# Tree stage: PE's transposes and outputs of a tile between the logits of the next, and ScalarE's activations and copies in turn

## The chip, the cores and the metric

The kernel runs on one core of a Trainium2 chip. The metric is the device time of one execution in microseconds (us). Engines by the profile's names: PE (TensorE) multiplies matrices and transposes, PEld are its weight loads, ACT is ScalarE, DVE is VectorE, POOL is GpSimd, SP issues transfers.

## The reference

Two layers over x of shape (2, 1024, 128). Each layer adds an attention and a feed-forward part of the normalised x to x. The second layer's feed-forward part is a forest of 8 binary trees of 255 nodes, and this stage alone is changed:

```python
logits = x @ W_in.T + b_in                      # 2048 rows, 8 * 255 = 2040 columns
decisions = (logits > 0)                        # per row, tree and node
acts = silu(logits)
# from the root, 7 times: go to the child that the node's decision names;
# dmap is 1 at the 8 nodes of a tree's path, 0 elsewhere
out = (acts * dmap).reshape(B, WIDTH) @ W_out.T # 2040 -> 128
```

## The kernel before

The program is a row of stages, each in a block of its own: the projections, attention and experts of layer 0, the projections of layer 1, the trees (`walk_trees`, lines 1999 to 2175), the attention of layer 1. No instruction of a stage runs beside another stage's.

The trees work on NT = 16 tiles of 128 rows. For tile t:

- POOL copies the 128 columns of the transposed input into `xt` (line 2039).
- PE computes the logits, 128 x 2040, into the four banks of `ps_l`, in four chunks of 512 columns (504 in the last). A chunk is a small bf16 product that adds the bias (line 2058) and the float32 product (line 2059, two passes). Two chunks are a half, and `l_ready` counts halves. There is only one `ps_l`: a half of the next tile waits until ACT has read this tile's (`silu_ready`).
- DVE compares a half with zero (line 2143, "decision", `dec_ready`), twice; then walks the path down the trees with 14 small products and differences (lines 2151 and 2152, "path"); then multiplies the activations by the path (line 2159, "mask", `masked`).
- ACT applies Silu to a half, from `ps_l` into `act_v` (line 2105), behind DVE's decision on the same half. `act_v` has two buffers, one for each of two tiles.
- PE transposes the masked activations, 16 blocks in four groups of four ("T0" to "T3", line 2072), into the two buffers of `ps_t` (`t_ready`). ACT copies each group to SBUF (`mT`, two buffers; lines 2113, 2115 and 2116: "copy 0" to "copy 3", `t_read`). PE multiplies the copied blocks by W_out and sums all 16 in `ps_f` (line 2083, "outputs 0" to "outputs 3"; four blocks are eight passes).
- DVE adds `ps_f` to x (line 2164).

Each engine has its instructions in one written order and waits on semaphores. The stage is turned by one tile: between tiles t-1 and t, PE's order is all four chunks of tile t, then transposes and outputs of tile t-1, which begin with a wait for its mask. ACT's order is both Silus of tile t, then the four copies of tile t-1. DVE's order is decisions, path and mask of tile t, then the addition of tile t-1. Two such sections stand in the body of a loop that turns seven times; the first section and the last outputs are written out. "Section t" below is the part that has the logits of tile t and the outputs of tile t-1.

Of the kernel before, what the change touches and what calls it, by code (L numbers as in the profile page):

```python
# [9 lines left out]
ACT = mybir.ActivationFunctionType  # L10
# [4 lines left out]
P = 128  # L15
B, S, D = 2, 1024, 128
NT = B * S // P
# [27 lines left out]
NCH = (WIDTH + P - 1) // P  # L45
LASTW = WIDTH - (NCH - 1) * P
# [1952 lines left out]
def walk_trees(nc, g):  # L1999

    with ExitStack() as ctx:
        r = Room(nc, ctx, "ff")
        win, wout, bin32 = g.win, g.wout, g.bin32
        rest = r.sb("rest", [1, WIDTH])
        binp = r.sb("binp", [1, 3, WIDTH], BF16)
        bins = r.sb("bins", [3, WIDTH], BF16)
        xt = r.sb("xt", [P, 2, P])
        dec = r.sb("dec", [P, PAR, NODES], BF16)
        path = r.sb("path", [P, PAR, NODES], BF16)
        act_v = r.sb("act_v", [P, 2, WIDTH])  # L2010
        mT = r.sb("mT", [P, 2, CH])
        ps_l = r.ps("ps_l", [P, 4 * CH])
        ps_t = r.ps("ps_t", [P, 2, CH])
        ps_f = r.ps("ps_f", [P, CH])

        w_in, bias_ready, step = r.sem("w_in"), r.sem("bias_ready"), r.sem("step")
        x_ready, l_ready, dec_ready, silu_ready = r.sem("x_ready"), r.sem("l_ready"), r.sem("dec_ready"), r.sem("silu_ready")
        masked, t_ready, t_read, f_ready, f_read = (r.sem("masked"), r.sem("t_ready"), r.sem("t_read"), r.sem("f_ready"),
                                                    r.sem("f_read"))
        NCK = (NCH + 3) // 4  # L2020
        STEPS = 2 * DEPTH - 1
        HALVES = [(0, 2 * CH), (2 * CH, WIDTH)]
        BOUNDS = [(c * CH, min(CH, WIDTH - c * CH)) for c in range(4)]

        with nc.Block() as block:
            @block.sync
            def _(sp):
                sp.wait_ge(bias_ready, 4)
                for part in range(3):
                    sp.dma_start(bins[part:part + 1, :], binp[0:1, part, :]).then_inc(w_in, 16)  # L2030
                sp.wait_ge(w_in, 48)
# [15 lines left out]
            @block.tensor  # L2047
            def _(pe):
                pe.wait_ge(g.trees_in, 64)
                pe.wait_ge(w_in, 48)  # L2050

                def logits(t, p, first):
                    pe.wait_ge(x_ready, t + 1)
                    for x in range(2):
                        if not (first and p == 0):
                            pe.wait_ge(silu_ready, t * 2 + (x - 1))
                        for c, w in BOUNDS[2 * x:2 * x + 2]:
                            pe.matmul(ps_l[:, c:c + w], g.onesb[0:3, :], bins[:, c:c + w], start=True, stop=False)
                            m = pe.matmul(ps_l[:, c:c + w], xt[:, p, :], win[:, c:c + w], start=False, stop=True)
                        m.then_inc(l_ready, 1)  # L2060

                def outputs(t, p, first):
                    pe.wait_ge(masked, t + 1)
                    if not (first and p == 0):
                        pe.wait_ge(f_read, t)

                    def turn(x):
                        if not (first and p == 0 and x < 2):
                            pe.wait_ge(t_read, t * NCK + (x - 1))
                        for c in range(4 * x, min(4 * x + 4, NCH)):  # L2070
                            w = P if c < NCH - 1 else LASTW
                            m = pe.transpose(ps_t[0:w, x % 2, (c % 4) * P:(c % 4 + 1) * P],
                                             act_v[:, p, c * P:c * P + w], g.ident[:, :])
                        m.then_inc(t_ready, 1)

                    turn(0)
                    for x in range(NCK):
                        if x + 1 < NCK:
                            turn(x + 1)
                        pe.wait_ge(t_read, t * NCK + (x + 1))  # L2080
                        for c in range(4 * x, min(4 * x + 4, NCH)):
                            w = P if c < NCH - 1 else LASTW
                            m = pe.matmul(ps_f[:, 0:P], mT[0:w, x % 2, (c % 4) * P:(c % 4 + 1) * P],
                                          wout[0:w, c, :], start=(c == 0), stop=(c == NCH - 1))
                        if x == NCK - 1:
                            m.then_inc(f_ready, 1)

                logits(0, 0, True)
                logits(1, 1, True)
                outputs(0, 0, True)  # L2090
                with pe.Fori(1, NT // 2) as i:
                    logits(i * 2, 0, False)
                    outputs(i * 2 - 1, 1, False)
                    logits(i * 2 + 1, 1, False)
                    outputs(i * 2, 0, False)
                outputs(NT - 1, 1, False)

            @block.scalar
            def _(act):
                def silu(t, p, first):  # L2100
                    if not first:
                        act.wait_ge(t_ready, (t - 1) * NCK)
                    for x, (lo, hi) in enumerate(HALVES):
                        act.wait_ge(dec_ready, t * 2 + (x + 1))
                        act.activation(act_v[:, p, lo:hi], ps_l[:, lo:hi], ACT.Silu).then_inc(silu_ready, 1)

                def turned(t, p, first):
                    for x in range(NCK):
                        act.wait_ge(t_ready, t * NCK + (x + 1))

                        full = 4 * P if x < NCK - 1 else (NCH - 1 - 4 * x) * P
                        if x < NCK - 1:
                            act.activation(mT[:, x % 2, 0:full], ps_t[:, x % 2, 0:full], ACT.Copy).then_inc(t_read, 1)
                        else:
                            act.activation(mT[:, x % 2, 0:full], ps_t[:, x % 2, 0:full], ACT.Copy)
                            act.activation(mT[0:LASTW, x % 2, full:full + P], ps_t[0:LASTW, x % 2, full:full + P],
                                           ACT.Copy).then_inc(t_read, 1)

                silu(0, 0, True)
                silu(1, 1, True)  # L2120
                turned(0, 0, True)
                with act.Fori(1, NT // 2) as i:
                    silu(i * 2, 0, False)
                    turned(i * 2 - 1, 1, False)
                    silu(i * 2 + 1, 1, False)
                    turned(i * 2, 0, False)
                turned(NT - 1, 1, False)

            @block.vector
            def _(dve):  # L2130
# [171 lines left out]
```

## Time and profile before

| | us |
|---|---|
| median of 3 runs | 2088.07 (2087.74 to 2088.33) |
| execution that was profiled | 2088.2 |
| its span | 2086.5 |
| the tree stage in it, from the first logits to the last addition | 827.32 to 1053.56 |

The page gives the kernel as a whole, with PE busy 84% of the span, DVE 72%, ACT 64% and POOL 30%. The tree stage is a ninth of the span, and none of its lines is among the costliest groups; it is read by windows and by the timeline of a stretch. In a timeline each line is a run of like instructions: start, duration, engine, line, operation, output and inputs, count, and in brackets how long the engine was idle ahead of it and what ended that. The durations of PE's groups overlap those of the next, so what PE needs for a group is read from start to start. PE's granted clock is a share of 2.4 GHz; its two levels are 1.0 and 0.5, and a mean between them is a mix.

### The profile page before, as it was taken

How to read it: one execution, taken by the hardware profiler on the slowest of the kernel's cores; microseconds unless marked ns; L12 is line 12 of the kernel's file. 1: busy time of each engine (PE TensorE's matmuls, PEld its weight loads, DVE VectorE, ACT ScalarE, POOL GpSimd, SP SyncE). 2: the span in 40 equal slices, each digit the busy share in tenths (PEclk: the TensorE clock that was granted, in tenths of full speed). 3: DMA queues.
4: the chain of work that ended last, by engine and by line, in shares of the span. 5: the costliest groups of instructions: out<-in, count | busy, mean ns of one | idle time of the engine just before them, and what ended most of it. 6: DMA issues, size and time to landing. Idle time of an engine off the chain costs nothing. (4 is left out here: it accounts for less than half of the span.)

```text
span 2086.5 us, 35986 instructions
## 1 busy us (share of the span) xinstructions
PE 1760.6 (84%) x10131; PEld 1056.3 (51%) x10163; DVE 1497.3 (72%) x4721; ACT 1327.3 (64%) x2819; POOL 619.0 (30%) x1540
## 2 busy tenths in 40 slices
PE   5699999999978895888865888888889838988877
PEld 2345555577756443555532555555555525555544
DVE  4588888311133555777747899999999969999974
ACT  3177777533321521233347999999999939999983
POOL 0045454000000441000014444444444414444440
PEclk8599999999985997999987999999999969999988
DMA  6200000100010220000020110111100101011000
GB/s 168 82 21 22 23 23 16 41 1 0 0 50 0 81 91 31 0 0 0 0 64 11 31 32 16 31 31 31 31 24 23 31 16 28 18 31 31 21 18 15
DMA packets 38186, 61.77 MB, mean 30 GB/s; under 512 B 10225, under 2 KB 15347, under 8 KB 38004
## 3 DMA queue, kind: packets, MB, share of 16 engines
q1 hardware_dynamic: 38069, 60.51, 9.8%
q8 instruction: 36, 0.59, 0.1%
q14 instruction: 81, 0.66, 0.1%
HBM read 34.14 MB, written 17.83 MB: 25 GB/s over the span
## 5 line engine op out<-in xcount | busy, mean ns | idle before, releaser
L1629 ACT ACTIVATE a_trash<-a_sc,a_search 128x1024 bf16<-128x1024 f32 (+7 forms) x768 | 586.2, 767 | 74.6 <-POOL a_search L1568 31.7
L1384 PE MATMUL a_ps_s<-a_k,a_q 128*128 128x512 f32 (+3 forms) x768 | 311.1, 520 | 64.4 <-DVE a_sc L1845 51.1
L1418 PE MATMUL a_ps_o<-a_kT,a_v 128*65 128x512 f32 (+3 forms) x768 | 287.5, 498 | 53.7 <-ACT a_kT L1646 52.5
L1402 PE MATMUL a_ps_t<-g_ident,a_sc 128*128 128x128 f32 x1152 | 228.5, 285 | 20.9 <-ACT a_kT L1646 18.9
L1845 DVE TENSOR_SCALAR_CACHE_REDUCE a_sc<-a_ps_s,g_search 128x1024 f32<-128x1024 f32 (+7 forms) x256 | 207.9, 812 | 23.3 <-PE a_ps_s L1386 16.1
L585 DVE TENSOR_REDUCE a_top<-a_ps_row 128x1 f32<-128x512 f32 (+3 forms) x384 | 196.7, 553 | 24.6 <-PE a_ps_row L423 18.9
L1384 PEld LDWEIGHTS a_ps_s<-a_k,a_q 128*128 128x128 f32 x768 | 132.3, 196 | 160.0 <-issue 100.6
L1805 DVE SCALAR_TENSOR_TENSOR a_below<-a_sc,a_found 128x768 f32<-128x768 f32 (+7 forms) x256 | 211.3, 835 | 1.1
L1404 PE MATMUL a_ps_t<-a_minus,a_short 128*128 128x128 bf16 x1152 | 211.8, 221 | 0.0
L1402 PEld LDWEIGHTS a_ps_t<-g_ident,a_sc 128*128 128x128 f32 x1152 | 164.5, 143 | 92.0 <-ACT a_kT L1646 47.1
L549 ACT ACTIVATE a_prob<-a_ps_col 128x1024 f32<-128x1024 f32 (+7 forms) x256 | 159.2, 650 | 68.7 <-PE a_ps_col L436 65.5
L1646 ACT ACTIVATE a_kT<-a_ps_t 128x512 f32<-128x512 f32 x288 | 162.0, 583 | 24.9 <-PE a_ps_t L1404 17.7
L1418 PEld LDWEIGHTS a_ps_o<-a_kT,a_v 128*65 128x65 f32 x768 | 89.0, 140 | 164.5 <-ACT a_kT L1646 103.3
L741 ACT ACTIVATE ex_hid<-ex_ps_h,le_b 128x512 f32<-128x512 f32 x128 | 87.5, 687 | 128.1 <-PE ex_ps_h L718 127.8
L1818 DVE MAX8 a_best<-a_below 128x8 f32<-128x160 f32 (+5 forms) x576 | 157.2, 328 | 1.1
L1629 ACT ACTIVATION_READ_ACCUMULATOR a_trash<-a_sc,a_search 128x1 f32 x768 | 148.0, 193 | 0.0
L792 DVE SCALAR_TENSOR_TENSOR l_acc<-ex_ps_y,l_comb,l_acc 128x128 f32 x112 | 31.9, 345 | 151.4 <-PE ex_ps_y L709 151.1
L1639 ACT ACTIVATE a_short<-a_sc,a_cutoff 128x128 bf16<-128x128 f32 (+2 forms) x192 | 110.8, 655 | 44.9 <-DVE a_cutoff L1865 44.9
L1404 PEld LDWEIGHTS a_ps_t<-a_minus,a_short 128*128 128x128 bf16 x1152 | 123.7, 107 | 19.4 <-issue 19.4
L709 PEld LDWEIGHTS ex_ps_y<-le_w,ex_hid 128*128 128x128 f32 x1024 | 118.7, 192 | 13.4 <-issue 13.4
L709 PE MATMUL ex_ps_y<-le_w,ex_hid 128*128 128x128 f32 x1024 | 118.8, 275 | 0.0
L420 PE MATMUL a_ps_row<-a_k,a_q 128*128 128x512 bf16 (+3 forms) x353 | 114.7, 335 | 4.8 <-DVE a_top L585 2.7
(267 smaller groups left out, 3336.1 us busy)
## 6 DMA issues: line engine op xcount, KB each, us to landing
a_v<-g_v SPq DMA_DIRECT2D x32, 260.0 KB, 2.3
q1turned<-p_full SPq DMA_DIRECT2D x32, 256.0 KB, 2.0
a_q<-q1turned SPq DMA_DIRECT2D x32, 256.0 KB, 3.6
a_k<-k1turned SPq DMA_DIRECT2D x32, 256.0 KB, 4.0
stack<-p_parts SPq DMA_DIRECT2D x24, 256.0 KB, 3.7
a_q<-stack SPq DMA_DIRECT2D x32, 96.0 KB, 2.2
a_k<-stack SPq DMA_DIRECT2D x32, 96.0 KB, 2.2
le_w<-d_w SPq DMA_DIRECT2D x1, 2048.0 KB, 8.5
```

The source lines that it names most:

```text
L549: act.activation(prob[:, p, PO[j]:PO[j] + S - j * P], ps_col[:, col_buffer(n, p, j), 0:S - j * P], ACT.Exp, scale=SCALE).then_inc(col_read, 1)
L585: dve.tensor_reduce(top[:, i, c:c + 1], ps_row[:, bank, 0:width], AX.X, ALU.max).then_inc(row_read, 1)
L709: m = pe.matmul(ps_y[:, e % 2, t, :], hid[:, e % 2, hc, t * P:(t + 1) * P], w2[:, e, hc, :], start=(hc == 0), stop=(hc == HC - 1))
L1384: pe.matmul(ps_s[:, j % 2, c:c + w], q[:, p, i * P:width], k[:, p, c:c + w], start=True, stop=True)
L1402: pe.matmul(out, columns(h, i)[:, c * P:(c + 1) * P], g.ident[:, :], is_transpose=True, start=True, stop=False)
L1404: m = pe.matmul(out, short[:, OFF[i] + c * P:OFF[i] + (c + 1) * P], minus[:, :], start=False, stop=True)
L1418: m = pe.matmul(ps_o[0:VW1, lo // HALF, (lo % HALF) * P:CH], v[:, p, c, :], kT[:, u % 2, a * P:b * P], start=(c == 0), stop=(c == LAST[lo ...
L1629: act.activation(trash[:, u % 2, 0:(i + 1) * P], columns(h, i), ACT.Sign, scale=-1.0, bias=trials[:, p, c, i:i + 1], accum_out=balance[:, ...
L1646: act.activation(kT[:, u % 2, :], ps_t[:, u % 2, :], ACT.Exp).then_inc(t_read, 1)
L1805: lane[i] = did(dve.scalar_tensor_tensor(lows(i), columns(hs, i), found[:, i:i + 1], columns(hs, i), ALU.is_le, ALU.mult))
L1818: did(dve.max(best[:, p, i, a, :], buf[:, a * w:(a + 1) * w]))
L1845: dve.tensor_scalar(columns(h + 1, i), ps_s[:, j % 2, 0:(i + 1) * P], shift.rearrange("p n i -> p (n i)"), None, ALU.subtract, ALU.max, ac ...
```

## The change

PE: the logits of tile t are split around the first transposes of tile t-1. After three of the four chunks PE waits for the mask of tile t-1 and makes T0; then comes the fourth chunk, then T1, outputs 0, T2, outputs 1, T3, outputs 2, outputs 3. The wait for `f_read` (the addition of the tile before) moves from ahead of the transposes to ahead of outputs 0. ACT: the copies of tile t-1 and the Silus of tile t take turns: copy 0, Silu 0, copy 1, Silu 1, copy 2, copy 3. The orders of DVE, POOL and SP, all buffers and all instructions stay. The first section is now like the others, with the four chunks of tile 1 split in the same way.

```diff
--- before.py
+++ after.py
@@ -2049,82 +2049,105 @@
                 pe.wait_ge(g.trees_in, 64)
                 pe.wait_ge(w_in, 48)
 
-                def logits(t, p, first):
+                def half(t, p, x):
+                    for c, w in BOUNDS[2 * x:2 * x + 2]:
+                        pe.matmul(ps_l[:, c:c + w], g.onesb[0:3, :], bins[:, c:c + w], start=True, stop=False)
+                        yield pe.matmul(ps_l[:, c:c + w], xt[:, p, :], win[:, c:c + w], start=False, stop=True)
+
+                def turn(t, p, first, x):
+                    if not (first and x < 2):
+                        pe.wait_ge(t_read, t * NCK + (x - 1))
+                    for c in range(4 * x, min(4 * x + 4, NCH)):
+                        w = P if c < NCH - 1 else LASTW
+                        m = pe.transpose(ps_t[0:w, x % 2, (c % 4) * P:(c % 4 + 1) * P],
+                                         act_v[:, p, c * P:c * P + w], g.ident[:, :])
+                    m.then_inc(t_ready, 1)
+
+                def output(t, p, first, x):
+                    if x == 0 and not first:
+                        pe.wait_ge(f_read, t)
+                    pe.wait_ge(t_read, t * NCK + (x + 1))
+                    for c in range(4 * x, min(4 * x + 4, NCH)):
+                        w = P if c < NCH - 1 else LASTW
+                        m = pe.matmul(ps_f[:, 0:P], mT[0:w, x % 2, (c % 4) * P:(c % 4 + 1) * P],
+                                      wout[0:w, c, :], start=(c == 0), stop=(c == NCH - 1))
+                    if x == NCK - 1:
+                        m.then_inc(f_ready, 1)
+
+                def logits(t, p, first, x, both):
                     pe.wait_ge(x_ready, t + 1)
-                    for x in range(2):
-                        if not (first and p == 0):
-                            pe.wait_ge(silu_ready, t * 2 + (x - 1))
-                        for c, w in BOUNDS[2 * x:2 * x + 2]:
-                            pe.matmul(ps_l[:, c:c + w], g.onesb[0:3, :], bins[:, c:c + w], start=True, stop=False)
-                            m = pe.matmul(ps_l[:, c:c + w], xt[:, p, :], win[:, c:c + w], start=False, stop=True)
-                        m.then_inc(l_ready, 1)
-
-                def outputs(t, p, first):
-                    pe.wait_ge(masked, t + 1)
-                    if not (first and p == 0):
-                        pe.wait_ge(f_read, t)
-
-                    def turn(x):
-                        if not (first and p == 0 and x < 2):
-                            pe.wait_ge(t_read, t * NCK + (x - 1))
-                        for c in range(4 * x, min(4 * x + 4, NCH)):
-                            w = P if c < NCH - 1 else LASTW
-                            m = pe.transpose(ps_t[0:w, x % 2, (c % 4) * P:(c % 4 + 1) * P],
-                                             act_v[:, p, c * P:c * P + w], g.ident[:, :])
-                        m.then_inc(t_ready, 1)
-
-                    turn(0)
-                    for x in range(NCK):
-                        if x + 1 < NCK:
-                            turn(x + 1)
-                        pe.wait_ge(t_read, t * NCK + (x + 1))
-                        for c in range(4 * x, min(4 * x + 4, NCH)):
-                            w = P if c < NCH - 1 else LASTW
-                            m = pe.matmul(ps_f[:, 0:P], mT[0:w, x % 2, (c % 4) * P:(c % 4 + 1) * P],
-                                          wout[0:w, c, :], start=(c == 0), stop=(c == NCH - 1))
-                        if x == NCK - 1:
-                            m.then_inc(f_ready, 1)
-
-                logits(0, 0, True)
-                logits(1, 1, True)
-                outputs(0, 0, True)
+                    if not first:
+                        pe.wait_ge(silu_ready, t * 2 + (x - 1))
+                    chunks = half(t, p, x)
+                    next(chunks)
+                    if both:
+                        next(chunks).then_inc(l_ready, 1)
+                    return chunks
+
+                def section(t, p, first):
+                    u, q = t - 1, 1 - p
+                    logits(t, p, False, 0, True)
+                    second = logits(t, p, False, 1, False)
+                    pe.wait_ge(masked, t)
+                    turn(u, q, first, 0)
+                    next(second).then_inc(l_ready, 1)
+                    turn(u, q, first, 1)
+                    output(u, q, first, 0)
+                    turn(u, q, first, 2)
+                    output(u, q, first, 1)
+                    turn(u, q, first, 3)
+                    output(u, q, first, 2)
+                    output(u, q, first, 3)
+
+                logits(0, 0, True, 0, True)
+                logits(0, 0, True, 1, True)
+                section(1, 1, True)
                 with pe.Fori(1, NT // 2) as i:
-                    logits(i * 2, 0, False)
-                    outputs(i * 2 - 1, 1, False)
-                    logits(i * 2 + 1, 1, False)
-                    outputs(i * 2, 0, False)
-                outputs(NT - 1, 1, False)
+                    section(i * 2, 0, False)
+                    section(i * 2 + 1, 1, False)
+                pe.wait_ge(masked, NT)
+                turn(NT - 1, 1, False, 0)
+                for x in range(NCK):
+                    if x + 1 < NCK:
+                        turn(NT - 1, 1, False, x + 1)
+                    output(NT - 1, 1, False, x)
 
             @block.scalar
             def _(act):
-                def silu(t, p, first):
-                    if not first:
+                def silu(t, p, first, x):
+                    lo, hi = HALVES[x]
+                    if x == 0 and not first:
                         act.wait_ge(t_ready, (t - 1) * NCK)
-                    for x, (lo, hi) in enumerate(HALVES):
-                        act.wait_ge(dec_ready, t * 2 + (x + 1))
-                        act.activation(act_v[:, p, lo:hi], ps_l[:, lo:hi], ACT.Silu).then_inc(silu_ready, 1)
-
-                def turned(t, p, first):
-                    for x in range(NCK):
-                        act.wait_ge(t_ready, t * NCK + (x + 1))
-
-                        full = 4 * P if x < NCK - 1 else (NCH - 1 - 4 * x) * P
-                        if x < NCK - 1:
-                            act.activation(mT[:, x % 2, 0:full], ps_t[:, x % 2, 0:full], ACT.Copy).then_inc(t_read, 1)
-                        else:
-                            act.activation(mT[:, x % 2, 0:full], ps_t[:, x % 2, 0:full], ACT.Copy)
-                            act.activation(mT[0:LASTW, x % 2, full:full + P], ps_t[0:LASTW, x % 2, full:full + P],
-                                           ACT.Copy).then_inc(t_read, 1)
-
-                silu(0, 0, True)
-                silu(1, 1, True)
-                turned(0, 0, True)
+                    act.wait_ge(dec_ready, t * 2 + (x + 1))
+                    act.activation(act_v[:, p, lo:hi], ps_l[:, lo:hi], ACT.Silu).then_inc(silu_ready, 1)
+
+                def turned(t, x):
+                    act.wait_ge(t_ready, t * NCK + (x + 1))
+                    full = 4 * P if x < NCK - 1 else (NCH - 1 - 4 * x) * P
+                    if x < NCK - 1:
+                        act.activation(mT[:, x % 2, 0:full], ps_t[:, x % 2, 0:full], ACT.Copy).then_inc(t_read, 1)
+                    else:
+                        act.activation(mT[:, x % 2, 0:full], ps_t[:, x % 2, 0:full], ACT.Copy)
+                        act.activation(mT[0:LASTW, x % 2, full:full + P], ps_t[0:LASTW, x % 2, full:full + P],
+                                       ACT.Copy).then_inc(t_read, 1)
+
+                def section(t, p, first):
+                    u = t - 1
+                    turned(u, 0)
+                    silu(t, p, first, 0)
+                    turned(u, 1)
+                    silu(t, p, first, 1)
+                    turned(u, 2)
+                    turned(u, 3)
+
+                silu(0, 0, True, 0)
+                silu(0, 0, True, 1)
+                section(1, 1, True)
                 with act.Fori(1, NT // 2) as i:
-                    silu(i * 2, 0, False)
-                    turned(i * 2 - 1, 1, False)
-                    silu(i * 2 + 1, 1, False)
-                    turned(i * 2, 0, False)
-                turned(NT - 1, 1, False)
+                    section(i * 2, 0, False)
+                    section(i * 2 + 1, 1, False)
+                for x in range(NCK):
+                    turned(NT - 1, x)
 
             @block.vector
             def _(dve):
```

## Rows read from the trace of the kernel before

**Rows 1.** The page: the span.

```profile
span 2086.5 us, 35986 instructions
```

**Rows 2.** Windows: busy us by engine (instructions), then PE's granted clock, DMA share, GB/s.

```profile
868.00:1046.00 178.00, 151.84 (x780) 98.56 (x779) 128.95 (x235) 55.58 (x91) 3.23 (x11) 0.96 0.00 0
...
881.02:895.82 14.80, 12.83 (x62) 8.73 (x61) 11.19 (x19) 4.28 (x7) 0.29 (x1) 0.88 0.00 0
...
844.00:854.00 10.00, 8.18 (x43) 7.73 (x44) 9.35 (x17) 4.28 (x7) 0.00 (x0) 0.58 0.00 0
```

**Rows 3.** Timeline, one section: start, duration, engine, line, operation [idle before <- releaser].

```profile
908.97 0.38 PE L2058 MATMUL ff_ps_l<-ff_bins,g_onesb 3*128 3x512 bf16 x1
...
913.09 0.38 PE L2058 MATMUL ff_ps_l<-ff_bins,g_onesb 3*128 3x504 bf16 x1
...
914.35 1.04 PE L2072 MATMUL ff_ps_t<-g_ident,ff_act_v 128*128 128x128 f32 x8
...
914.55 1.22 DVE L2143 TENSOR_SCALAR ff_dec<-ff_ps_l 128x1016 bf16<-128x1016 f32 x1 [1.50 <-PE ff_ps_l L2059]
...
915.80 1.02 ACT L2105 ACTIVATE ff_act_v<-ff_ps_l 128x1016 f32<-128x1016 f32 x1 [1.70 <-DVE ff_dec L2143]
...
916.71 1.08 ACT L2113 ACTIVATE ff_mT<-ff_ps_t 128x512 f32<-128x512 f32 x2
...
917.36 1.16 PE L2083 MATMUL ff_ps_f<-l_wout,ff_mT 128*128 128x128 f32 x8 [1.97 <-ACT ff_mT L2113]
...
918.35 0.60 PE L2072 MATMUL ff_ps_t<-g_ident,ff_act_v 128*128 128x128 f32 x4
...
919.68 0.60 PE L2072 MATMUL ff_ps_t<-g_ident,ff_act_v 128*128 128x128 f32 x4
...
920.12 2.07 PE L2083 MATMUL ff_ps_f<-l_wout,ff_mT 128*128 128x128 f32 x16
...
920.32 0.49 ACT L2115 ACTIVATE ff_mT<-ff_ps_t 128x384 f32<-128x384 f32 x1 [0.73 <-PE ff_ps_t L2072]
...
921.20 2.29 DVE L2159 TENSOR_TENSOR ff_act_v<-ff_act_v,ff_path 128x2040 f32<-128x2040 f32 x1
...
922.12 0.38 PE L2058 MATMUL ff_ps_l<-ff_bins,g_onesb 3*128 3x512 bf16 x1
```

**Rows 4.** Timeline of the stage's start, to the first transposes of tile 1.

```profile
827.32 0.58 PE L2058 MATMUL ff_ps_l<-ff_bins,g_onesb 3*128 3x512 bf16 x1 [17.03 <-DMA ff_bins<-ff_binp]
...
829.83 0.60 PE L2058 MATMUL ff_ps_l<-ff_bins,g_onesb 3*128 3x512 bf16 x1
...
841.62 2.28 DVE L2159 TENSOR_TENSOR ff_act_v<-ff_act_v,ff_path 128x2040 f32<-128x2040 f32 x1
...
843.96 1.97 PE L2072 MATMUL ff_ps_t<-g_ident,ff_act_v 128*128 128x128 f32 x8 [3.52 <-DVE ff_act_v L2159]
...
849.62 1.06 PE L2072 MATMUL ff_ps_t<-g_ident,ff_act_v 128*128 128x128 f32 x4
...
850.47 1.91 PE L2083 MATMUL ff_ps_f<-l_wout,ff_mT 128*128 128x128 f32 x8
...
852.18 0.69 PE L2072 MATMUL ff_ps_t<-g_ident,ff_act_v 128*128 128x128 f32 x4
...
860.10 1.04 PE L2072 MATMUL ff_ps_t<-g_ident,ff_act_v 128*128 128x128 f32 x8
```

**Rows 5.** Timeline of the stage's end.

```profile
1037.64 1.04 PE L2072 MATMUL ff_ps_t<-g_ident,ff_act_v 128*128 128x128 f32 x8
...
1044.51 2.28 DVE L2159 TENSOR_TENSOR ff_act_v<-ff_act_v,ff_path 128x2040 f32<-128x2040 f32 x1
...
1047.09 1.06 PE L2072 MATMUL ff_ps_t<-g_ident,ff_act_v 128*128 128x128 f32 x8 [1.61 <-DVE ff_act_v L2159]
...
1053.27 0.29 DVE L2164 TENSOR_TENSOR g_x<-g_x,ff_ps_f 128x128 f32<-128x128 f32 x1 [6.29 <-PE ff_ps_f L2083]
```

**Rows 6.** Line 2105 of ScalarE: table loads, ns min/median/max, first and last start.

```profile
L2105 ACT ACT_TABLE_LOAD  x1: 1283/1283/1283, 816.2 to 816.2; - x1
```

## The prediction

> **What bounds the kernel now.** The page first: its span is 2086.5 us [rows 1], and none of the stage's lines is among its costliest groups. So I cut out the stage with the view of windows: from 868 to 1046 us PE is busy 151.8 of 178 us, DVE 129.0, ACT 55.6 [rows 2]. No engine is full, so the order of the work sets the time. The timeline of one section shows that order [rows 3]. At 908.97 PE starts the logits of a tile; the last of four chunks starts at 913.09, and the transposes of the tile before at 914.35. Then PE idles 1.97 us, to 917.36, until ACT has copied the first transposes. That copy stands on ACT behind both Silu halves, the second Silu waits for DVE's second decision (914.55 to 915.80), and this waits for the last logits. After the copy PE works without a real break, to the next logits at 922.12: 13.15 us for a tile. DVE idles ahead of that second decision, 1.50 us, for the same logits. The loop PE, DVE, ACT, PE is closed, and closes once a tile.
>
> Not every tile takes 13.15. The section from 881.02 takes 14.80, with a mean granted clock of 0.88 [rows 2], so 0.12 x 14.80 / 0.5 = 3.6 us of it at 1.2 instead of 2.4 GHz. It lies right behind the wait for the copy. From the first transposes of tile 1 (860.10) to those of tile 14 (1037.64) there are 13 intervals: 177.54 us, or 13.66 each [rows 4, 5]. 13 x 13.15 is 170.95, and the other 6.59 is four times the excess of 1.65 us: four sections had the slow stretch. The rest of the kernel lies in blocks of its own before and behind this one, and the next block's first loads are issued after this stage's last addition (1053.56) [rows 5]: nothing of it can hide in this stage or be hidden by it.
>
> **The change part by part.** No instruction is added or removed: a tile has the same 16 transposes, 32 output passes, four chunks, two Silus and five copies. No DMA moves. All durations therefore come from rows of before, and the sum is one of order. It is made against this profile's own execution (2088.2 us, its span and 1.7 around it), which lies 0.1 over the median of the runs.
>
> I call a the start of a section's first transposes.
>
> *DVE's branch.* The last chunk of logits now follows the first transposes, and these wait for the mask of the tile before. First transposes: 0.44 us for four (919.68 to 920.12). Start of a chunk to start of the decision on it: 1.46 (913.09 to 914.55). Decision and path together 6.65 (914.55 to 921.20), of which the decision is 1.25, to the start of its Silu at 915.80; the mask 2.29 [rows 3]. From the mask's end to the transposes that wait for it: 0.06 at one place (843.90 to 843.96), 0.30 at another (1046.79 to 1047.09, behind the end of the loop) [rows 4, 5]; I take 0.10, since inside the loop PE stands at the wait already. Sum: 0.44 + 1.46 + 6.65 + 2.29 + 0.10 = 10.94 us. The first decision (1.25, after an addition of 0.29 [rows 5]) fits between the mask's end and a + 1.90, with some 0.4 us idle; its logits were done at the section's start. This is the wait that the change adds: behind PE's wait for the mask now stand the last chunk and all outputs, and DVE's second decision waits for that chunk. On ACT, copy 0 now stands ahead of Silu 0, which so waits for the mask too; who needs Silu 0 (the next tile's logits, the mask) is 5 us away or more. POOL's copy of the input tile is allowed a tile ahead as before and costs nothing.
>
> *PE's branch.* T0 0.44, last chunk 1.26 (913.09 to 914.35), T1 0.44, outputs 0 0.99 (917.36 to 918.35), T2 and outputs 1 1.33 (918.35 to 919.68), T3 0.44, outputs 2 and 3 2.00 (920.12 to 922.12, with a small wait for the last copy in it), then three chunks of the next tile, 1.37 + 1.37 + 1.26 = 4.00 (a third of 908.97 to 913.09 is 1.37) [rows 3]. Sum 10.90. This holds if no copy is late. From the start of four transposes to the copy: 0.64 us (919.68 to 920.32). Copy 0: a + 0.64 to a + 1.24; outputs 0 start at a + 2.14, so the stall of 1.97 us is gone. Silu 0 starts behind the first decision, at a + 1.5, done at a + 2.5; copy 1 (transposes at a + 1.70) to about a + 3.1, needed at a + 3.57. Silu 1 starts with the end of the second decision, a + 3.15, to a + 4.15; copy 2 to a + 4.75, needed at a + 4.90: the narrowest place, 0.15 us. Copy 3 as now. PE is then at the next wait at a + 10.90 and the mask is done at a + 10.84: both engines are at their limit, and what is late next is either, by a few hundredths.
>
> So an interval is 10.94 us where the trace has 13.15 to 14.80. Its bounds: 10.90 with the short release; 11.14 with the long one; 11.3 if copy 2 besides misses its time by 0.15. The nearest rows give the short one, so I stay at 10.94.
>
> *The clock.* PE's idle time in a section falls from about 2.0 us in one piece to some 0.1 to 0.2 in two or three. The low stretches began right behind that piece, so I expect none of the four: that gain is in the 10.94. Should they stay, PE has no reserve to hide them, and 4 x 1.65 = 6.6 us are lost again.
>
> *Start.* Transposes of tile 0 still wait for its mask (843.96), with a longer idle ahead of them (PE stops one chunk earlier), and the clock is low there: 0.58 from 844 to 854 [rows 2]. At that clock four transposes take 0.85 (849.62 to 850.47), eight output passes 1.71 (to 852.18), a chunk 2.51 (827.32 to 829.83) [rows 4]. New section 1: 0.85 + 2.51 + 0.85 + 1.71 + 0.85 + 1.71 = 8.5, at 852.4, where the clock rose in the trace; then 0.44 + 2.0 and three chunks (4.0): transposes of tile 1 at 858.9, 1.2 us before 860.10. The last chunk of tile 1 is late by this (decision at 847.4, not 845), but its mask ends at 856.4, early enough. If PE's unbroken work brings the clock up sooner, up to 2.5 us more; if later, up to 1 less.
>
> *End.* Before, the last section's transposes and those of tile 15 are 9.45 us apart (1037.64 to 1047.09); now this is an interval like the others, a loss that stands in the sum by counting 14 intervals. The tail from 1047.09 to the end of the last addition, 1053.56, is 6.47 and unchanged [rows 5].
>
> *Sum.* 858.9 + 14 x 10.94 + 6.47 = 1018.5, against 1053.56: 35.0 us. 2088.2 - 35.0 = 2053.2 us; against the median it is 2053.1.
>
> **The rivals.**
> *The low clock stays in the loop (0.10).* For it: four of 14 sections have it, and section 1 is entered after a longer idle. Against: all four start behind a wait of 2 us that goes. Time: 2053.2 + 6.6 = 2059.8 us.
> *The hand-overs cost more (0.08).* Three engines now pass work within tenths of a microsecond; each late copy hits PE. With 0.5 us more an interval, 11.44: 2060.2 us. Against it: the hand-overs of rows 3 are of this kind already (the second decision is over at 915.77, its Silu starts at 915.80).
> *ScalarE reloads tables (0.02).* A section now goes between Silu and Copy four times, not twice. A load took 1.28 us [rows 6]. Two would stand between the second decision and copy 2: 2.56 less the margin of 0.15 is 2.4 an interval, 14 x 2.4 = 34: 2087 us, no change. Against it: one load in the whole stage for 32 Silus, and a Copy starts with no gap at the Silu's end (915.80 + 1.02, copy at 916.71).
> The Trainium skill ("ScalarE: Activation LUTs", section "What ACT_TABLE_LOAD costs") puts a switch of sets at 2.66 us with the drain, by which two would add 5.3 us to an interval and make the kernel slower by some 37 us; its section on table sets has Copy in every set, and with that the trace agrees.
> *The other side: PE sinks to the low clock for the stage (0.02).* The wait for the mask now stands in the middle of the logits, in every section, and section 1 begins cold. At 1.2 GHz a section is 4 x 2.51 + 4 x 0.85 + 4 x 1.71 = 20.3 us, 14 of them 284 against the 187.0 between 860.10 and 1047.09: 2185 us. It decides from a mean interval of (187.0 + 1.2) / 14 = 13.44, that is when over a quarter of the sections (2.5 of 9.4 us) run so. Against it: PE at the low clock would be busy without a break, and in the trace it rose in just such a stretch (844 to 854).
> That the change doesn't do what it says (an order on PE undone elsewhere) has no mechanism here: the queues take the order as written.
>
> **How the numbers follow.** 0.78 for the forecast, 0.10, 0.08, 0.02 and 0.02 for the rivals. Low end: 2050.5, the interval of 10.90 and 2 us more at the start. High end: 2061, which takes in either of the first two rivals (2059.8 and 2060.2), since the margin at copy 2 is small beside what the hand-overs leave open. A change within 0.2% (4 us, what can't be told from none here) has 0.02, slower 0.02, faster 0.96.
>
> **What would show it.** Right: starts of the first transposes 10.9 to 11.0 us apart; no wait of PE for a copy above some 0.2; DVE idle only about 0.4 us before the second decision; granted clock 1.00 from the second section on; the stage's last addition near 1018.6. Wrong: intervals of 11.3 and more with PE waiting for copy 1 or 2; sections with 0.88; table loads; or later stages that take longer than before, for which I see no cause.

## The result, and the profile after

The changed kernel takes 2055.09 us (median of 4 runs, 2052.08 to 2057.55), the one before 2088.20 (4 runs, 2087.74 to 2088.66). The ratio is 0.9841, with a 95% interval of 0.9824 to 0.9858: 33.1 us less, where 35.0 were forecast, and inside the range.

The page of the changed kernel: span, and busy time of each engine.

```profile
span 2050.4 us, 36006 instructions
...
PE 1755.8 (86%) x10163; PEld 1048.2 (51%) x10163; DVE 1495.6 (73%) x4721; ACT 1328.5 (65%) x2819; POOL 620.8 (30%) x1540
```

The busy times are those of before to 5 us in 1760 (PE), the span is 36.1 us shorter [rows 1]: what went was waiting and low clock. Where it went is read from the stage's windows; the columns are as in [rows 2].

```profile
core 0: us, PE busy (x) PEld busy (x) DVE busy (x) ACT busy (x) POOL busy (x), PEclk, DMA share, GB/s
...
860.00:1000.00 140.00, 139.81 (x754) 88.49 (x753) 122.99 (x228) 53.26 (x88) 3.26 (x11) 1.00 0.00 0
...
842.60:847.50 4.90, 4.85 (x14) 2.98 (x15) 2.32 (x2) 1.85 (x3) 0.30 (x1) 0.50 0.00 0
...
1011.50:1015.00 3.50, 3.46 (x16) 3.16 (x17) 0.19 (x1) 1.19 (x2) 0.00 (x0) 0.52 0.02 5
...
826.08:1019.25 193.17, 183.77 (x960) 116.01 (x960) 156.01 (x288) 69.29 (x112) 4.15 (x14) 0.96 0.00 0
```

From the first logits to the last addition the stage takes 193.17 us, 33.07 less than the 226.24 of before. The other two rows show where its clock is low: in section 1 (0.50 from 842.60 to 847.50) and at the last tile (0.52). The other 3.0 us of the span's difference lie outside the stage: it begins 1.24 earlier, and what follows it takes 1031.15 instead of 1032.94. No instruction differs there, and such differences come and go between the profiles of the kernels below. Between 860 and 1000 us the granted clock is 1.00; between 868 and 1046 it was 0.96 [rows 2].

One section of the changed kernel, in its timeline (start, duration, engine, line, operation, and in brackets the idle time before it):

```profile
907.49 0.39 PE L2054 MATMUL ff_ps_l<-ff_bins,g_onesb 3*128 3x512 bf16 x1
...
909.24 2.28 DVE L2182 TENSOR_TENSOR ff_act_v<-ff_act_v,ff_path 128x2040 f32<-128x2040 f32 x1
...
911.66 0.65 PE L2062 MATMUL ff_ps_t<-g_ident,ff_act_v 128*128 128x128 f32 x4
...
912.24 0.38 PE L2054 MATMUL ff_ps_l<-ff_bins,g_onesb 3*128 3x504 bf16 x1
...
912.35 0.60 ACT L2128 ACTIVATE ff_mT<-ff_ps_t 128x512 f32<-128x512 f32 x1 [6.00 <-PE ff_ps_t L2062]
...
912.89 1.03 ACT L2122 ACTIVATE ff_act_v<-ff_ps_l 128x1024 f32<-128x1024 f32 x1
...
913.50 0.60 PE L2062 MATMUL ff_ps_t<-g_ident,ff_act_v 128*128 128x128 f32 x4
...
913.70 1.22 DVE L2166 TENSOR_SCALAR ff_dec<-ff_ps_l 128x1016 bf16<-128x1016 f32 x1 [0.84 <-PE ff_ps_l L2055]
...
913.94 1.06 PE L2072 MATMUL ff_ps_f<-l_wout,ff_mT 128*128 128x128 f32 x8
...
914.96 1.02 ACT L2122 ACTIVATE ff_act_v<-ff_ps_l 128x1016 f32<-128x1016 f32 x1 [0.22 <-DVE ff_dec L2166]
...
915.87 0.59 ACT L2128 ACTIVATE ff_mT<-ff_ps_t 128x512 f32<-128x512 f32 x1
...
916.60 2.07 PE L2072 MATMUL ff_ps_f<-l_wout,ff_mT 128*128 128x128 f32 x16
...
918.60 0.39 PE L2054 MATMUL ff_ps_l<-ff_bins,g_onesb 3*128 3x512 bf16 x1
```

None of PE's lines has a bracket: the wait of 1.97 us before outputs 0 (913.94 here) is gone [rows 3]. A short wait for the mask is left ahead of T0, 0.2 us, too short for a bracket. The transposes T0, at 900.54, 911.66 and 922.76, are 11.11 us apart, and so are 12 of the 14 intervals to 0.02. ACT does copy, Silu, copy, Silu, copy, and its own waits (6.00 and 0.22 us) hold up neither PE nor DVE. The loop now runs through DVE: mask to 911.52, T0 at 911.66, last chunk at 912.24, second decision at 913.70, path, and the next mask.

The stage's start (section 1) and its end:

```profile
842.65 1.11 PE L2062 MATMUL ff_ps_t<-g_ident,ff_act_v 128*128 128x128 f32 x4 [4.87 <-DVE ff_act_v L2182]
...
843.70 0.60 PE L2054 MATMUL ff_ps_l<-ff_bins,g_onesb 3*128 3x504 bf16 x1
...
846.07 1.06 PE L2062 MATMUL ff_ps_t<-g_ident,ff_act_v 128*128 128x128 f32 x4
...
855.94 0.60 PE L2062 MATMUL ff_ps_t<-g_ident,ff_act_v 128*128 128x128 f32 x4
```

```profile
1011.54 1.97 PE L2062 MATMUL ff_ps_t<-g_ident,ff_act_v 128*128 128x128 f32 x8 [4.00 <-DVE ff_act_v L2182]
...
1013.44 1.81 PE L2072 MATMUL ff_ps_f<-l_wout,ff_mT 128*128 128x128 f32 x8
...
1018.96 0.29 DVE L2187 TENSOR_TENSOR g_x<-g_x,ff_ps_f 128x128 f32<-128x128 f32 x1 [7.27 <-PE ff_ps_f L2072]
```

Transposes of tile 1 start 29.86 us after the first logits (32.78 before). Those of tile 15 start behind 4.00 us of idle time, at a granted clock of 0.52, and eight passes take 1.81 us; from them to the end it is 7.71 us, where it was 6.47 [rows 5].

### The profile page after: what moved, and what is told of

Its sections match the earlier page's. It is cut to its first block and busy times, and to the rows that moved or that the text cites. A ratio compares the mean times of both kernels' runs of the same rounds, so it can differ in the third digit from the quotient of the medians.

```text
span 2050.4 us, 36006 instructions
## 1 busy us (share of the span) xinstructions
PE 1755.8 (86%) x10163; PEld 1048.2 (51%) x10163; DVE 1495.6 (73%) x4721; ACT 1328.5 (65%) x2819; POOL 620.8 (30%) x1540
## 5 line engine op out<-in xcount | busy, mean ns | idle before, releaser
L420 PE MATMUL a_ps_row<-a_k,a_q 128*128 128x512 bf16 (+3 forms) x384 | 124.2, 342 | 4.9 <-DVE a_top L585 2.7
L385 POOL TENSOR_SCALAR_AFFINE_SELECT a_prob<-a_prob 128x128 f32<-128x128 f32 x256 | 75.6, 296 | 144.6 <-POOLq L382 144.1
```

What stands on the lines that cost most here:

```text
L420: last = pe.matmul(ps_row[:, bank, 0:width], q[:, h, i * P:(i + 1) * P], k[:, h, c * CH:c * CH + width], start=True, stop=True)
```

## The experiments

All profiles are read by the same four numbers, in us: first logits to T0 of tile 1, interval between T0s in the loop, T0 of tile 15 to the end, and the whole stage. The kernel before was run alongside each series, with medians of 2088.20, 2087.84 and 2087.03 us; a ratio goes with the runs of its own series, so it isn't the quotient of two medians of this table.

| kernel | to T0 of tile 1 | interval | last tile | stage | median (runs) | ratio to before, 95% |
|---|---|---|---|---|---|---|
| before | 32.78 | 13.15, four of 14.80 | 6.47 | 226.24 | 2088.20 (4) | 1 |
| changed | 29.86 | 11.11 | 7.71 | 193.17 | 2055.09 (4) | 0.9841 (0.9824 to 0.9858) |
| changed, again | 33.32 | 11.12 | 7.88 | 196.88 | 2055.25 (5) | 0.9847 (0.9834 to 0.9861) |
| PE's order alone | 36.24 | 13.59, two of 16.31 and 15.15 | 6.56 | 234.74 | 2093.56 (8) | 1.0026 (1.0016 to 1.0037) |
| ACT's order alone | 30.06 | 11.51 | 7.58 | 196.66 | 2057.31 (4) | 0.9866 (0.9851 to 0.9882) |
| before, wait filled | 32.99 | 13.15, none longer | 7.55 | 220.96 | 2081.45 (8) | 0.9974 (0.9963 to 0.9985) |
| path without its last level | 29.10 | 10.91 | 8.20 | 188.58 | 2050.07 (2) | 0.9827 |
| without outputs 1 | 29.52 | 11.11 | 7.26 | 192.33 | 2054.01 (2) | 0.9846 |
| mask in halves | 30.71 | 10.91 | 7.77 | 190.30 | 2050.90 (5) | 0.9830 (0.9816 to 0.9843) |
| mask in halves, PE kept warm | 24.76 | 10.92 | 6.56 | 183.17 | 2043.26 (5) | 0.9792 (0.9778 to 0.9805) |

### Which of the two orders carries it

```diff
 # PE's order alone: ACT of the changed kernel as it was before
-                    turned(u, 0)
                     silu(t, p, first, 0)
-                    turned(u, 1)
                     silu(t, p, first, 1)
+                    turned(u, 0)
+                    turned(u, 1)
                     turned(u, 2)
```

> PE in the new order, ACT in the old one (both Silus, then the four copies). My theory, that the stall goes only if copy 0 no longer stands behind Silu 1: the second decision now comes later than before (behind T0), Silu 1 runs from a + 3.3 to a + 4.2, copy 0 to a + 4.8, so outputs 0 start 2.5 us later than in the changed kernel; an interval is 11.1 + 2.5 = 13.6 us, as long as before, and the low clock is there again in some sections. Time 2088 to 2096 us. Rival, PE's order carries the gain by itself: interval 11.1 to 11.5, time 2055 to 2061 us.

PE's timeline in this kernel:

```profile
899.74 0.38 PE L2054 MATMUL ff_ps_l<-ff_bins,g_onesb 3*128 3x512 bf16 x1
...
905.55 0.60 PE L2062 MATMUL ff_ps_t<-g_ident,ff_act_v 128*128 128x128 f32 x4
...
908.56 1.16 PE L2072 MATMUL ff_ps_f<-l_wout,ff_mT 128*128 128x128 f32 x8 [2.41 <-ACT ff_mT L2128]
...
913.33 0.39 PE L2054 MATMUL ff_ps_l<-ff_bins,g_onesb 3*128 3x512 bf16 x1
```

The wait for copy 0 has grown from 1.97 to 2.41 us, and an interval is 13.59 (logits start at 899.74 and at 913.33). Two sections had the low clock. The time is 0.26% above before, interval 0.16 to 0.37%: PE's new order by itself is a small loss. The rival is out.

The other half: the kernel before with the changed kernel's whole ACT block (copy 0, Silu 0, copy 1, Silu 1, copy 2, copy 3).

> ACT in the new order, PE in the old one (four chunks, then T0 and T1). My theory: outputs 0 need only copy 0, done at a + 1.24, against T1's end at a + 0.88, so 0.4 us of the stall of 1.97 is left; outputs 1 and 2 wait some tenths for copies 1 and 2, which stand behind the Silus. Interval 11.6 us, DVE idle twice a tile, no low clock, time 2060 to 2064 us: three quarters of the gain. Rival, each order is worth nothing without the other: interval 13.1 or more, time 2080 to 2090 us.

```profile
912.48 1.04 PE L2072 MATMUL ff_ps_t<-g_ident,ff_act_v 128*128 128x128 f32 x8
...
913.12 0.60 ACT L2111 ACTIVATE ff_mT<-ff_ps_t 128x512 f32<-128x512 f32 x1 [7.16 <-PE ff_ps_t L2072]
...
913.62 1.02 ACT L2105 ACTIVATE ff_act_v<-ff_ps_l 128x1024 f32<-128x1024 f32 x1
...
913.77 1.16 PE L2083 MATMUL ff_ps_f<-l_wout,ff_mT 128*128 128x128 f32 x8 [0.25 <-ACT ff_mT L2111]
...
915.00 1.04 ACT L2105 ACTIVATE ff_act_v<-ff_ps_l 128x1016 f32<-128x1016 f32 x1
...
915.89 0.63 ACT L2111 ACTIVATE ff_mT<-ff_ps_t 128x512 f32<-128x512 f32 x1
```

T0 and T1 start at 912.48, copy 0 at 913.12, Silu 0 behind it, outputs 0 at 913.77 after 0.25 us. The interval is 11.51, no section is long, and 2057.31 us were measured, somewhat better than the 2060 to 2064 expected. So ACT's order alone takes 1.64 of the 2.04 us of an interval and all of the low clock in the loop; PE's split of the logits adds the other 0.40, and only beside it. By medians the two kernels are 2 us apart and their 95% ranges overlap, so the times alone don't separate them. The traces do: each of 13 intervals is 0.40 longer with ACT's order alone, 5.2 us. But its last one is 1.57 shorter (9.44 against 11.01 us), because PE's old order has the last tile's logits all done ahead of the T0 that this interval is counted from, and so the two stages are 3.5 us apart (196.66 and 193.17).

### What the clock was worth

```diff
+                        if x == 0:
+                            pe.matmul(ps_w[:, :], g.ident[:, :], win[:, 0:CH], start=True, stop=True)
+                            for _ in range(2):
+                                pe.matmul(ps_w[:, :], g.onesb[0:3, :], bins[:, 0:CH], start=True, stop=True)
                         pe.wait_ge(t_read, t * NCK + (x + 1))
```

> The kernel before, with one float32 product of 512 columns and two small bf16 ones put on PE in front of outputs 0, results unused: they fill most of PE's wait of 1.97 us for copy 0. My theory, that this wait brings the low clock of four sections: all sections take 13.15 us, the stage 226.2 - 6.6 = 219.6 us, the time 2081.5 us, and 6.6 of the changed kernel's 33 us are the clock's. Rival, the low stretches have nothing to do with the wait (or the products overrun it): three to five long sections stay, time 2088 us or more.

First the kernel before, around its wait for copy 0 in the section from 881.02 (the wait ends at 889.4; columns as in [rows 2]):

```profile
886.00:890.00 4.00, 2.03 (x15) 1.51 (x13) 3.09 (x10) 2.15 (x4) 0.29 (x1) 0.99 0.00 0
889.90:893.30 3.40, 3.40 (x18) 3.40 (x18) 3.19 (x7) 0.60 (x1) 0.00 (x0) 0.50 0.00 0
```

PE's timeline of one section with the wait filled, and the window of the loop:

```profile
913.21 1.02 PE L2082 MATMUL ff_ps_w<-l_win,g_ident 128*128 128x512 f32 x2
...
914.17 0.60 PE L2084 MATMUL ff_ps_w<-ff_bins,g_onesb 3*128 3x512 bf16 x2
...
915.34 1.16 PE L2088 MATMUL ff_ps_f<-l_wout,ff_mT 128*128 128x128 f32 x8 [0.58 <-ACT ff_mT L2118]
```

```profile
860.00:1034.00 174.00, 165.91 (x845) 98.22 (x844) 130.75 (x243) 57.44 (x94) 3.55 (x12) 1.00 0.00 0
```

The extra products run from 913.21 to about 914.8 and outputs 0 wait 0.58 instead of 1.97 us. All 13 intervals are 13.15 us, the granted clock is 1.00, and the kernel is 0.26% faster for doing more work. The four long sections (6.6 us in the profile of before) were thus the wait's doing, through the clock. The time is the 2081.5 us forecast. The stage gained 5.3 us, because its last tile took 1.1 longer: there PE waited only 0.25 us for copy 0, and the extra products hold up outputs 0.

### What sets 11.11 us

```diff
 # path without its last level
-                    for d in range(DEPTH):
+                    for d in range(LEVELS):          # LEVELS = DEPTH - 1
```

> The changed kernel without the last of the seven levels of the path on DVE (two operations of 0.77 us a tile; the lowest nodes' part of the path is left at 1). My theory, that DVE's branch sets the interval of 11.11 and PE's is 0.2 behind it: the interval falls to PE's own sum, 0.53 + 1.26 + 0.44 + 0.89 + 0.44 + 0.89 + 0.44 + 2.00 + 1.38 + 1.37 + 1.26 = 10.90, not by the 1.55 taken away. Rival, PE binds already: it stays at 11.11. Second rival, PE is far from binding: 9.6.

```profile
900.39 0.60 PE L2063 MATMUL ff_ps_t<-g_ident,ff_act_v 128*128 128x128 f32 x4
...
902.38 1.22 DVE L2167 TENSOR_SCALAR ff_dec<-ff_ps_l 128x1016 bf16<-128x1016 f32 x1 [1.94 <-PE ff_ps_l L2056]
...
911.31 0.60 PE L2063 MATMUL ff_ps_t<-g_ident,ff_act_v 128*128 128x128 f32 x4
```

The interval is 10.91 to 10.92 (900.39 to 911.31 here), DVE has 1.94 us of idle time before its second decision, and PE is the loop: 1.55 us less on DVE bring 0.20.

```diff
 # without outputs 1
-                    for c in range(4 * x, min(4 * x + 4, NCH)):
+                    for c in range(4 * x, min(4 * x + 4, NCH)) if x != 1 else ():
```

> The changed kernel without the eight passes of outputs 1 on PE (0.89 us a tile). My theory: DVE's branch has nothing of them, the interval stays at 11.11 and PE waits some 1.0 us for the mask. Rival, PE binds: 10.2.

```profile
907.61 2.05 PE L2072 MATMUL ff_ps_f<-l_wout,ff_mT 128*128 128x128 f32 x16 [0.64 <-ACT ff_mT L2128]
...
909.59 0.39 PE L2054 MATMUL ff_ps_l<-ff_bins,g_onesb 3*128 3x512 bf16 x1
...
911.44 2.29 DVE L2182 TENSOR_TENSOR ff_act_v<-ff_act_v,ff_path 128x2040 f32<-128x2040 f32 x1
...
913.86 0.65 PE L2062 MATMUL ff_ps_t<-g_ident,ff_act_v 128*128 128x128 f32 x4
```

Without eight of its passes PE has 0.89 us less to do, yet T0s are 11.11 apart and T0 still comes 0.13 behind the mask's end (911.44 + 2.29 to 913.86). The wait for the mask is not the 1.0 us expected: 0.64 us of PE's new idle time goes to copy 2, since outputs 2 now follow T3 directly, and some 0.3 to the mask. Neither costs anything. Together: DVE's branch sets 11.11, and PE's limit is 10.91, 0.20 below.

### A version that beats both

```diff
-                    a = act_v[:, p, :]
-                    dve.tensor_tensor(a, a, path.rearrange("p a n -> p (a n)"), ALU.mult).then_inc(masked, 1)
+                    for x, (lo, hi) in enumerate(HALVES):
+                        dve.wait_ge(silu_ready, t * 2 + (x + 1))
+                        a = act_v[:, p, lo:hi]
+                        dve.tensor_tensor(a, a, path.rearrange("p a n -> p (a n)")[:, lo:hi],
+                                          ALU.mult).then_inc(masked, 1)
 ...
+                    if x in (0, 2):                  # ahead of T0 and of T2
+                        pe.wait_ge(masked, t * 2 + (1 + x // 2))
```

> The changed kernel with DVE's mask in two halves, so that T0 and T1 wait for the first 1024 columns alone, T2 for the rest. If DVE's branch binds by the wait of T0 for the whole mask, its loop shrinks by 1.1 us to 10.0, DVE's own work is 10.35, and PE's sum of 10.90 takes over: interval 10.90, stage 14 x 0.21 = 2.9 us shorter and 1.1 more at the last tile, time some 4 us below the changed kernel, 2051 us. Rival, the halves cost DVE more than they free (another 0.1 us and a hand-over on each): interval 11.1 to 11.2, no gain.

DVE and PE in this kernel:

```profile
921.65 2.35 DVE L2183 TENSOR_TENSOR ff_act_v<-ff_act_v,ff_path 128x1024 f32<-128x1024 f32 x2
...
923.92 0.60 PE L2064 MATMUL ff_ps_t<-g_ident,ff_act_v 128*128 128x128 f32 x4
```

T0 no longer waits (923.92, with the first half of the mask done about 1.1 us before), and PE's 10.91 is the interval. The halves cost DVE 2.35 us for two where one mask took 2.28. The median is 2050.90; beside the changed kernel's 2055.25 that is the expected 4 us, but the 95% ranges of the two ratios overlap, so the gain rests on the timeline: 0.2 us in each of 13 intervals and 1.1 in the last (11.01 to 9.92), 3.8 us in all. The stages of the changed kernel's two profiles are 2.9 and 6.6 us longer than this one; what differs from 3.8 is mostly the start.

```diff
+                def warm(n):
+                    for _ in range(n):
+                        pe.matmul(ps_w[:, :], g.ident[:, :], win[:, 0:CH], start=True, stop=True)
 ...
+                warm(8)        # ahead of the wait for the biases, before the first logits
+                    warm(3)    # section 1, ahead of T0
+                warm(2)        # ahead of T0 of tile 15
```

> As the kernel with the mask in halves, and float32 products of 512 columns, results unused, on PE where it has nothing to do: 8 ahead of the first logits, 3 ahead of T0 in section 1, 2 ahead of the last tile's T0. If the low clock at the start and the end of the stage comes from PE's idle time there: the first two chunks 1.37 instead of 2.5 us, T0, last chunk and T1 of section 1 at full clock (2 us), the tail 6.5 instead of 7.7: 5 us less, time 2046 us, and a narrower spread, since the start of the stage was what differed between the two profiles of the changed kernel (29.9 and 33.3 us from the first logits to T0 of tile 1). Rival, the products delay what waits behind them, or the clock falls all the same: no gain or a loss against the kernel with halves.

PE's timeline at the start of this kernel's stage (the unread products start at 816.21), and the window of its last T0:

```profile
816.21 9.92 PE L2052 MATMUL ff_ps_w<-l_win,g_ident 128*128 128x512 f32 x16 [5.94 <-PEq L870]
...
827.26 0.38 PE L2060 MATMUL ff_ps_l<-ff_bins,g_onesb 3*128 3x512 bf16 x1 [1.13 <-DMA ff_bins<-ff_binp]
...
828.63 0.39 PE L2060 MATMUL ff_ps_l<-ff_bins,g_onesb 3*128 3x512 bf16 x1
...
840.76 0.66 PE L2070 MATMUL ff_ps_t<-g_ident,ff_act_v 128*128 128x128 f32 x4 [1.26 <-DVE ff_act_v L2192]
...
852.02 0.60 PE L2070 MATMUL ff_ps_t<-g_ident,ff_act_v 128*128 128x128 f32 x4
```

```profile
1003.80:1007.00 3.20, 2.79 (x23) 2.58 (x24) 1.34 (x3) 1.18 (x3) 0.00 (x0) 1.00 0.00 0
```

The first chunk takes 1.37 us (827.26 to 828.63) where it took 2.51 [rows 4], T0 of tile 1 comes at 24.76 instead of 30.71 us, and the last tile takes 6.56 instead of 7.77 at clock 1.00. The stage is 7.1 us shorter than with the halves alone, the median 7.6, more than the 5 expected: the start alone brought 6.0. It begins at full clock, and DVE's decisions come earlier with the logits. Part of it is chance: in the profile with the halves alone PE's clock stayed low for 12 us of the start, as in the changed kernel's second profile below, and not for 5 as in its first. At 2043.26 us this version is 2.1% below the kernel before (1.95 to 2.2%).

### Where the spread of the times comes from

> The changed kernel once more, for a second profile and its spread. Theory A, the spread of its times (2052.08 to 2057.55, where the kernel before has 2087.74 to 2088.66) comes from the stages behind the trees, which start at another moment in each execution relative to when the clock is taken down: the tree stage is 193.2 us within 1 in this profile, and the span's difference lies outside it. Rival B, it comes from the tree stage, which may have one or more sections at the low clock: the stage is longer by 1.5 or 3 us where the span is.

The question rests on the first four runs of the kernel before, and more runs take it back: 26 further ones lie between 2082.44 and 2092.20 us, wider than the nine of the changed kernel (2052.08 to 2057.55). These runs don't show that the change made the time less steady. What is left is where two profiles of one kernel differ.

The second profile's span is 2055.1, 4.7 us above the first. Its stage is 3.7 longer, its loop the same (11.12): 3.5 of it lie in the start, 0.2 in the last tile. The window of the first logits:

```profile
826.50:839.00 12.50, 12.42 (x15) 2.99 (x15) 3.27 (x7) 1.99 (x2) 0.30 (x1) 0.51 0.00 0
```

Here the clock stayed low for the first 12.5 us of PE's work, to 839; in the first profile chunks took 1.37 us from 830.87 on. Theory A is wrong for these two profiles, and B too in its letter: it is the stage's start, not a section in the loop. One us of the 4.7 is outside the stage. What makes the stretch behind the stage differ by over 6 us between kernels (1027.7 to 1033.9) was not tried; a difference of a few us between two medians of the table can come from there.

## Why the prediction was right

**The time.** Stage and medians both gained 33.1 us, against 35.0 forecast. That they agree so closely is partly chance: by the second profile the stage gained 29.4.

**The stall.** The step that outputs 0 need only copy 0, and copy 0 only T0, held as written: 1.97 us gone, copy 2 in time (915.87 to 916.46, outputs 2 at 916.60). That the gain needs ACT's order above all was not in the prediction; it took both as one.

**DVE's branch as the loop** held. The term that was mis-sized is T0 to the last chunk: 0.44 was taken from transposes followed by outputs, and with logits behind them it is 0.53 without a wait (855.94 to 856.47) and 0.58 behind one. The release was 0.14, not 0.10. 0.58 + 1.46 + 6.65 + 2.28 + 0.14 = 11.11, against 10.94: 14 x 0.17 = 2.4 us. One sign came out otherwise: DVE idles 0.84 us before the second decision, not some 0.4. The way to that decision is 0.18 longer (0.14 in T0 and 0.04 in the release), and addition and first decision take 1.34 us from the mask's end, not 1.54.

**PE's branch** was forecast at 10.90 and measured at 10.91, when it alone was the bound. That is chance in part: T0 is 0.09 longer and outputs 0, without a wait ahead of them, 0.10 shorter than the rows said.

**The clock in the loop.** None of the four low stretches is left, and filling the wait in the kernel before shows the cause. In the profile of before, 6.6 of the 33 us are this.

**The start** was forecast with 1.2 us of gain and up to 2.5 more; the first profile has 2.9, the second a loss of 0.5. The second is outside what was allowed for (a gain of 0.2 at least): the prediction left the moment of the clock's rise open in section 1, but not at the very start, where in the second profile five chunks ran at the low clock and not two. The two profiles differ by that moment, 830.9 and 839.1.

**The end** is the step that failed: the tail of 6.47 us did not stay unchanged. Behind the last chunk of logits PE now needs 6.4 us for its outputs, not 9.0, while DVE needs as long as before for the mask. So PE idles 4.00 us ahead of the last T0 instead of 1.61 [rows 5]; the clock falls and the tail costs 1.24 more. The other kernels bear this out: with 2.4 to 4.1 us of idle time there, the low clock fell into the tail and it took 7.3 to 8.2 us; with 1.26 to 1.61 us it ran at full clock (6.47 to 6.56 us, and 7.55 with the filling products in the way). The sum for the first profile: 35.0 + 1.7 (start) - 2.4 (intervals) - 1.24 (end) = 33.1.

**The rivals.** One table load in the stage again, for twice as many changes between Silu and Copy. The hand-overs and the longer T0 cost 0.17 an interval together, not 0.5. PE's low clock for the stage: none in the loop.

The Trainium skill ("TensorE: Matmul & The Clock Gate", section "HAM oscillation") says that a kernel whose PE idles between its pieces of work falls back to the half clock again and again. The traces agree in kind: with a wait of 1.97 us in each of them, four of 14 sections took 14.80 us, and none when the wait was filled.

## What to carry to other kernels

When an engine hands work on in a ring, write down for each engine what the other waits for and put that first: here ACT's new order, with a copy of 0.6 us moved ahead of the Silus, was worth 1.6 us a tile, while the more visible change on PE alone lost time. After such a change look for the new loop by making one engine's work shorter at a time; it shows how far the next limit is before anything is built for it. And look at PE's idle time at a stage's start and end: in these traces it was paid twice, the second time as half clock, and products whose result nobody reads brought 7 us.

## What the hardware showed that was not expected

A wait of only 1.97 us in 13.15 was enough for the low clock to come back, in four of 14 sections and not in the others; with 0.58 us it did in none. The four are not scattered: they are the third, sixth, ninth and twelfth interval. The length of the wait alone doesn't decide it either: with 2.41 us in each section (PE's order alone) two sections had the low clock. Which sections it falls in was not tried. A kernel that does more on PE (the filled wait, 2081.45 us) is faster than the one that doesn't (2087.84). At the stage's start PE worked 4.8 us at the low clock in one execution (826.08 to 830.87) and 12.5 us in another, with the same instructions.
